# Order of the routing arithmetic in two routed layers: slots' experts, maximum and shift after the one-hot rows, one-hot rows in four parts

## The reference

```python
# first layer; x is the layer-normalised input, 800 tokens
logits = xf @ router_w + router_b
probs = softmax(logits)
top_p, top_i = top_k(probs, 2)
top_p = top_p / sum(top_p)
gates[t, top_i] += top_p
h = silu(x @ w1[e]) * (x @ w3[e])
out = sum over e of gates[t, e] * (h @ w2[e])
# second layer: 8 experts, W1, W2, W3, softmax over the two best logits
x = x + tanh(g_ffn[layer]) * out
```

## Time and profile before

| | us |
|---|---|
| median of 3 runs | 2107.54 |
| lowest and highest run | 2104.54, 2107.74 |
| the profiled execution | 2116.41 |
| its span, first to last instruction | 2114.7 |
| TensorE busy in the span (matmuls) | 1932.6 (91%) |
| VectorE busy | 1022.1 (48%) |
| ScalarE busy | 842.6 (40%) |
| GpSimd busy | 659.5 (31%) |

### The profile page before, as it was taken

The page is one execution under the profiler, slowest core; times in us unless marked ns, Lnnn a source line. Parts: engine busy times, 40 slices in busy tenths (PEclk is TensorE's granted clock), DMA queues, the critical chain, the costliest instruction groups (busy, mean ns, idle before and its releaser), DMA issues. The chain is left out here.

```text
span 2114.7 us, 35637 instructions
## 1 busy us (share of the span) xinstructions
PE 1932.6 (91%) x12328; PEld 1570.0 (74%) x12328; DVE 1022.1 (48%) x2243; ACT 842.6 (40%) x1792; POOL 659.5 (31%) x555
## 2 busy tenths in 40 slices
PE   5889999999999999999859999999997885999983
PEld 3568878787777778787648888888884665999983
DVE  6324555555555545544464323333335656554544
ACT  3223443433434443434434323333323534655540
POOL 4011020303030111200034445555422104787872
PEclk9899999999999999999969999999998986999997
DMA  7630101010011102000053213333349125545546
GB/s 207 205 122 1 54 14 52 19 52 19 30 33 35 37 9 59 12 17 17 5 177 120 94 66 113 111 105 109 119 154 314 33 87 168 167 172 167 191 140 205
DMA packets 111912, 201.58 MB, mean 95 GB/s; under 512 B 31520, under 2 KB 32320, under 8 KB 111252
## 3 DMA queue, kind: packets, MB, share of 16 engines
q1 hardware_dynamic: 106964, 183.93, 26.5%
q0 software_dynamic: 4800, 15.73, 2.2%
HBM read 171.64 MB, written 27.98 MB: 94 GB/s over the span
## 5 line engine op out<-in xcount | busy, mean ns | idle before, releaser
L461 POOL TENSOR_TENSOR a_rows<-a_rows,a_gain_x 128x512 f32<-128x512 f32 (+1 forms) x48 | 68.3, 1422 | 555.8 <-DVE a_rows L876 555.8
L620 PE MATMUL a_kv_ps<-a_kvin_hi,a_wk_hi 128*128 128x512 f32 (+1 forms) x512 | 196.2, 383 | 1.0 <-DVE a_kvin_lo L883 1.0
L1094 PE MATMUL f_banks<-f_wab_hi,f_x_hi 128*128 x448 | 185.4, 414 | 1.3 <-DVE f_x_lo L1766 1.3
L621 PE MATMUL a_kv_ps<-a_kvin_lo,a_wk_hi 128*128 128x512 f32 (+1 forms) x512 | 180.4, 352 | 0.0
L622 PE MATMUL a_kv_ps<-a_kvin_hi,a_wk_lo 128*128 128x512 f32 (+1 forms) x512 | 180.3, 352 | 0.0
L1096 PE MATMUL f_banks<-f_wab_hi,f_x_lo 128*128 x448 | 177.1, 395 | 0.0
L1095 PE MATMUL f_banks<-f_wab_lo,f_x_hi 128*128 x448 | 175.8, 392 | 0.0
L543 ACT ACTIVATE a_probs<-a_probs,a_neg_max 100x822 f32<-100x822 f32 x128 | 125.9, 984 | 113.1 <-DVE a_neg_max L907 112.9
L1788 DVE TENSOR_TENSOR f_h_sb<-f_h_sb,f_banks 128x256 f32<-128x256 f32 x112 | 47.2, 422 | 244.4 <-ACT f_h_sb L1511 243.4
L1511 ACT ACTIVATE f_h_sb<-f_banks 128x256 f32<-128x256 f32 x112 | 43.0, 384 | 294.1 <-PE f_banks L1096 294.1
L1094 PE MATMUL m_banks<-m_wab_hi,m_x_hi 128*128 x512 | 155.8, 304 | 2.5 <-DVE m_x_lo L1766 1.7
(11 more groups left out here) (411 smaller groups left out, 4876.0 us busy)
## 6 DMA issues: line engine op xcount, KB each, us to landing
f_raw<-f_pieces SPq DMA_DIRECT2D x94, 256.0 KB, 2.7
m_raw<-m_pieces SPq DMA_DIRECT2D x92, 256.0 KB, 2.8
f_wab_raw<-f_pieces SPq DMA_DIRECT2D x42, 512.0 KB, 6.3
m_wab_raw<-m_pieces SPq DMA_DIRECT2D x42, 512.0 KB, 6.4
a_rows<-ctx SPq DMA_DIRECT2D x8, 1280.0 KB
ahead_piece<-g_ctx SPq DMA_DIRECT2D x2, 2880.0 KB, 19.2
a_wout_sb<-L_xattn_Wkv SPq DMA_DIRECT2D x8, 512.0 KB, 15.4
m_y_acc<-m_pieces SPq DMA_DIRECT2D x8, 512.0 KB, 6.2
```

Source lines behind the costliest of these rows:

```text
L461: own.link(nc.gpsimd.tensor_tensor(row, row, gain_x[0:n, :], ALU.mult))
L620: nc.tensor.matmul(out, hi_l, hi_r, start=first, stop=False)
L621: nc.tensor.matmul(out, hi_l, lo_r, start=False, stop=False)
L1094: nc.tensor.matmul(out, left_hi, right_hi, start=start, stop=False)
```

## The change

In `gated_experts`, so in both layers:

- VectorE's two comparisons come ahead of the wait for constants; the wait, now for 5, stands behind them, ahead of the first use of `before`.
- The maximum and the shift (two instructions) and the slots' experts (three) are taken from their places and put behind the one-hot rows, ahead of the first four splits.
- The one-hot rows are made by four instructions of 4 x 128 columns, where two made 8 x 128, and TensorE waits for each of the four.
- TensorE waits for the slots' experts behind the row matmuls, and loads all of them there.

```diff
@@ TensorE @@
-            pe.wait_ge(expert_done, 1)
...
-            slot_expert = [expert_of(s) for s in range(EARLY)]
             for i in range(B * TOP):
-                if i % B == 0:
-                    pe.wait_ge(at_row_done, i // B + 1)
+                if i % (B // 2) == 0:
+                    pe.wait_ge(at_row_done, i // (B // 2) + 1)
...
             ins.then_inc(rows_ready, 1)
-            slot_expert += [expert_of(s) for s in range(EARLY, CORE)]
+            pe.wait_ge(expert_done, 1)
+            slot_expert = [expert_of(s) for s in range(CORE)]
@@ VectorE @@
-            dve.wait_ge(const_done, 4)
...
             nc.vector.tensor_tensor(above[0:M, :, :, :], other, this, ALU.is_gt)
             own.link(nc.vector.tensor_tensor(equal[0:M, :, :, :], other, this, ALU.is_equal))
+            dve.wait_ge(const_done, 5)
...
-            own.link(nc.vector.tensor_reduce(l_max[0:M, :], logits[0:M, :, :], axis=AX.X, op=ALU.max))
-            nc.vector.tensor_tensor(p_exp[0:M, :, :], ..., ALU.subtract).then_inc(shift_done, 1)
...
-            own.link(nc.vector.tensor_tensor(passed, ..., ALU.is_ge))
-            own.link(nc.vector.tensor_reduce(expert_f, passed, axis=AX.X, op=ALU.add))
-            nc.vector.tensor_scalar(expert[:, 0:SLOTS], expert_f[0:1, :], float(E - 1), None, ALU.min).then_inc(expert_done, 1)
...
-            ROWS = [M, B, P]
-            for n in range(TOP):
-                i = slice(B * n, B * n + B)
+            HB = B // 2
+            ROWS = [M, HB, P]
+            for n in range(0, B * TOP, HB):
+                i = slice(n, n + HB)
                 nc.vector.tensor_tensor(at_row[0:M, i, :], row_at[0:M, :].unsqueeze(1).to_broadcast(ROWS),
                                         passing[:, i].unsqueeze(2).to_broadcast(ROWS), ALU.is_equal).then_inc(at_row_done, 1)
+            own.link(nc.vector.tensor_tensor(passed, ..., ALU.is_ge))
+            own.link(nc.vector.tensor_reduce(expert_f, passed, axis=AX.X, op=ALU.add))
+            nc.vector.tensor_scalar(expert[:, 0:SLOTS], expert_f[0:1, :], float(E - 1), None, ALU.min).then_inc(expert_done, 1)
+            own.link(nc.vector.tensor_reduce(l_max[0:M, :], logits[0:M, :, :], axis=AX.X, op=ALU.max))
+            nc.vector.tensor_tensor(p_exp[0:M, :, :], ..., ALU.subtract).then_inc(shift_done, 1)
```

More of the change, by code:

```diff
@@ L1691, in _ @@
             nc.vector.tensor_scalar(picked, rank[0:M, :, :], TOP - 0.5, None, ALU.is_lt).then_inc(chosen_done, 1)
-            own.link(nc.vector.tensor_reduce(l_max[0:M, :], logits[0:M, :, :], axis=AX.X, op=ALU.max))
-            nc.vector.tensor_tensor(p_exp[0:M, :, :], logits[0:M, :, :], l_max[0:M, :].unsqueeze(2).to_broadcast([M, B, E]), ALU.subtract).then_inc(shift_done, 1)
             dve.wait_ge(iota_ready, 1)
@@ L1719, in _ @@
             own.link(nc.vector.tensor_tensor(end, start, count, ALU.add))
-            own.link(nc.vector.tensor_tensor(passed, iota[:, 0:SLOTS].unsqueeze(2).to_broadcast([P, SLOTS, E]), end.unsqueeze(1).to_broadcast([P, SLOTS, E]), ALU.is_ge))
-            own.link(nc.vector.tensor_reduce(expert_f, passed, axis=AX.X, op=ALU.add))
-            nc.vector.tensor_scalar(expert[:, 0:SLOTS], expert_f[0:1, :], float(E - 1), None, ALU.min).then_inc(expert_done, 1)
             own.link(nc.vector.tensor_tensor(pos[0:M, :, :], banks[0:M, POS, 0:B * E].rearrange("p (b e) -> p b e", e=E),
@@ L1741, in _ @@
             own.link(nc.vector.tensor_tensor(by_batch, by_batch.bitcast(F32), token_of[0:M, :].unsqueeze(2).unsqueeze(3).to_broadcast([M, B, TOP, SLOTS]), ALU.mult))
-            ROWS = [M, B, P]
-            for n in range(TOP):
-                i = slice(B * n, B * n + B)
+            HB = B // 2
+            ROWS = [M, HB, P]
+            for n in range(0, B * TOP, HB):
+                i = slice(n, n + HB)
                 nc.vector.tensor_tensor(at_row[0:M, i, :], row_at[0:M, :].unsqueeze(1).to_broadcast(ROWS),
                                         passing[:, i].unsqueeze(2).to_broadcast(ROWS), ALU.is_equal).then_inc(at_row_done, 1)
+            own.link(nc.vector.tensor_tensor(passed, iota[:, 0:SLOTS].unsqueeze(2).to_broadcast([P, SLOTS, E]), end.unsqueeze(1).to_broadcast([P, SLOTS, E]), ALU.is_ge))
+            own.link(nc.vector.tensor_reduce(expert_f, passed, axis=AX.X, op=ALU.add))
+            nc.vector.tensor_scalar(expert[:, 0:SLOTS], expert_f[0:1, :], float(E - 1), None, ALU.min).then_inc(expert_done, 1)
+            own.link(nc.vector.tensor_reduce(l_max[0:M, :], logits[0:M, :, :], axis=AX.X, op=ALU.max))
+            nc.vector.tensor_tensor(p_exp[0:M, :, :], logits[0:M, :, :], l_max[0:M, :].unsqueeze(2).to_broadcast([M, B, E]), ALU.subtract).then_inc(shift_done, 1)
             def split(q, g, c):
```

## The result

The changed kernel takes 2109.76 us (median of 20 runs, 2106.10 to 2113.95), the kernel before 2106.82 (20 runs beside them, 2103.51 to 2111.30). The medians lie 2.9 us apart; the ratio on record, which isn't the quotient of the medians, is 1.0016, 95% interval [1.0010, 1.0023]: 3.4 us slower (2.1 to 4.8). The change is clear of the noise, but under the 0.2% at which the forecast counts a change. The forecast was 2112.4, 4.9 more than before. The profiled execution took 2109.37 us, span 2107.6; it is 7.1 us shorter than the profiled one of before, where the medians say longer, so single spans don't compare here.

The account below looks back on a forecast made before the run. TensorE's list was taken to bound both routed layers from its first token on. Later starts of 1.7 and 3.2 us sum to +4.9 on 2107.5, giving 2112.4 us; own range 2111 to 2113.5, eight times in ten 2106 to 2115.

Parts of the forecast that it names:

- The comparisons' wait: VectorE's opening comparisons without a wait for constants: 0 gain, bounds 0 and 0.1 us per layer.
- Rows sooner, cast unmoved: First layer: row matmuls end 1.46 us sooner, but VectorE's splits hold the row cast, so gathers come only 0.1 us sooner.
- Rival C: Gathers come with the row matmuls' end and loads are hidden: 3.2 us sooner in sum, 2104.3 us; chance 0.04.
- The loads: TensorE's 14 (16) register loads behind the row matmuls, 0.643 us each: first products 1.7 and 3.2 us later, 4.9 in sum.
- The prediction's signs: Trace marks: matmuls end near 1084.7, cast within 0.2 us of 1086.1, loads from 1083.5 and 1754.3, turning where they end.
- The price by the Trainium skill's 200 ns: At about 200 ns per register load, 14 take 2.8 us and 16 take 3.2, so the change would cost nothing.
- rival B: TensorE's loads are hidden, each near 0.2 us or beside other work; only 0.1 per layer stays: 2107.3 us; chance 0.05.
- The clock: TensorE's clock rise from the 1.2 GHz level during the first layer's first products: taken as 0, kept at +-0.8 us.
- The sum: Both layers' later starts of TensorE's products, 1.7 and 3.2 us, together +4.9 us: 2112.4 us.
- rival A: An existing wait, ScalarE's 8.0 us for the second slot's hidden result, swallows the delay: +0 to +1.7, 2108.4 us; chance 0.27.
- one microsecond of the kernel: Each microsecond TensorE's list starts later costs the kernel one in either routed layer, unless a later wait swallows it.
- Rival D: Dearer than the sum: TensorE's clock costs 0.8 us in the first layer and more in the second; 2115 us; chance 0.07.

Follow-up runs that it names:

- cast_first: The changed kernel with VectorE's row cast ahead of the first four splits, loads as in the changed kernel; 2110.11 us, ratio to the kernel before 1.0016.
- spread_cast_first: loads_spread with VectorE's row cast ahead of the first four splits; 2108.33 us, ratio to the kernel before 1.0015.
- loads_late: The kernel before with only TensorE's wait for the experts and all register loads put behind the row matmuls; 2122.26 us, ratio to the kernel before 1.0021.
- loads_spread: The changed kernel with two loads ahead of the first turning, each later slot's behind its tokens' turning; ratios to the kernel before 1.0002, repeated 0.9990.
- loads_double: The changed kernel with every expert number loaded twice behind the row matmuls; 2129.78 us, ratio to the kernel before 1.0065.

## Why the prediction was right, and where its sizes were off

**The comparisons' wait.** Forecast 0. L1683 starts at +0.72 in the first layer, L1686 did at +0.73; in the second 0.72 against 0.84. Right to 0.12 us.

**Rows sooner, cast unmoved.** Forecast end of the matmuls 1084.67, on before's clock +13.70; measured +13.72. Forecast cast 0.1 (first) and 0.1 to 0.2 (second) sooner; measured 0.09 and 0.20. The reason was incomplete: I had the gathers wait for the cast behind the splits, and cast_first shows that they would have waited for the splits also without it. Rival C is closed by that, too: spread_cast_first has its conditions, early cast and no block of loads, and 1.0015 instead of its 0.9985.

**The loads.** The term that decides. Their start was forecast at +12.54 and +15.70; measured +12.5 and +15.6. Turning forecast 2.4 and 3.6 later; measured 2.73 and 3.54. The first layer's step was (1090.7 - 1082.0) / 13 = 0.669 instead of 0.643, 0.36 us over 14 of them. L1094 forecast 1.7 and 3.2 later; measured 2.05 and 3.10. The prediction's signs (where the row matmuls, the cast and the loads stand, and the turning where the loads end) all came true. loads_late and loads_spread show that this is the term, and that the rest of the change is worth nothing measurable.

**The price by the Trainium skill's 200 ns** (Runtime: NRT & Kernel Launch, Instruction fetch mechanics), and with it rival B, 2107.3, is out: the load alone took 0.30 us (median of 14 and of 16), the step 0.65 to 0.67.

**The clock.** Forecast 0 with +-0.8; in the profile 0.55 of the first layer's delay was back by the second slot's products, and the clock rose ahead of them.

**The sum.** Forecast 4.9, path 5.15, measured 3.4 (2.1 to 4.8). It lies between the forecast and rival A's upper end of 1.7, and the time, 2109.76, is inside the range of 2106 to 2115 but below the forecast's own 2111 to 2113.5. That wide range holds rivals A and B as well, so being inside it says little for the sum; and of the two outcomes "slower" (0.45) and "same" (0.48), on a line drawn at 0.2%, it was the second. Less the clock's 0.55, 4.6 would remain, inside the interval; A's hold was seen to swallow the second layer's delay in one profile, to be absent in others, and to move the first layer too. The prediction named the sign for this itself, a first wait of TensorE that is shorter by the delay: in the first layer its waits went from 1.43 to 0.41 us. So the mis-sized term is "one microsecond of the kernel" for each by which TensorE's list starts later: 0.66 of it was passed on (3.4 / 5.15; by the interval 0.41 to 0.93), 0.77 in loads_late and 0.53 between the changed kernel and loads_double. How the rest divides between clock and hold isn't settled, and the kept profiles can't settle it. Rival D didn't occur.

## What to carry to other kernels

When an instruction is moved behind another, its queue's own work moves with it: look at what the queue did in the wait that you shorten. Register loads at 0.65 us each were free while TensorE waited for VectorE; six of them moved behind that wait put the turning 2.7 and 3.5 us later. Spread one by one between the slots they cost nothing that could be measured. And a result that is ready sooner buys nothing until the engine that must act on it is free; here the first GpSimd gather also ended no sooner than about 1 us after VectorE's list had.

## What the runs showed of the hardware

- The first gather's 1.13 us on GpSimd became 2.81 beside three VectorE subtractions, 2.26 beside two, and 1.94 with four where its wait took part of them; most later gathers beside such instructions stayed at 0.95, the longest took 1.45.
- A constant written by GpSimd beside VectorE's sooner comparison took longer, too. GpSimd after, second layer; the same took 0.29 us before:

```profile
1736.26 0.80 POOL L1434 TENSOR_SCALAR_AFFINE_SELECT m_scratch<-m_scratch 128x128 f32<-128x128 f32 x1
```

- ScalarE read TensorE's finished second-slot products late in seven of the thirteen profiles (3.1 to 5.2 us after their end in the first layer, 3.7 to 10.8 in the second), and at once or within 0.7 us in the other six. In the second layer of four it was let go within 0.4 us of the last gather packet, in three 2.0 to 7.0 us ahead of it. What holds it stays open.
- Delaying the turning in loads_double stretched the gathers as well: VectorE's list stands at the low half of the first slot, and a gather waits for a split behind it. GpSimd there, second layer:

```profile
1783.29 1.16 POOL L1457 DMA_INDIRECT m_y_acc<-m_xn,m_rows_at  x1 [11.28 <-DVE m_wab_lo L1750]
```
